# The expert gates' inverse root and exponential: from GpSimd's power to ScalarE's Sqrt and Exp

## The chip, the cores and the metric

One core of a Trainium2 chip. The program is one launch that computes two layers of a network on 8192 tokens of 256 channels. The metric is the device time of one execution in microseconds (us), smaller is better.

## The reference, cut to what matters

Each of the two layers ends with a feed-forward part in which a graph attention scores four experts for every token, and the two best experts are mixed:

```python
agg = segment_sum(msg, dst).reshape(M, HEADS * NUM_EXPERTS) + b_gat
scores = _layernorm(agg, ln_gamma, ln_beta).reshape(M, HEADS, NUM_EXPERTS).mean(1)
# _layernorm: (x - mu) * rsqrt(var + LN_EPS) * g + b      LN_EPS = 1e-5
topk_s, topk_i = jax.lax.top_k(scores, TOP_K)             # TOP_K = 2 of 4
w = jax.nn.softmax(topk_s, axis=-1)
for ei in range(NUM_EXPERTS):
    g = jnp.where(topk_i == ei, w, 0.0).sum(-1)
    hh = jax.nn.gelu(x @ W1[ei] + b1[ei], approximate=False)
    out = out + g[..., None] * (hh @ W2[ei] + b2[ei])
x = x + out
```

The change touches two values of this: 1 / sqrt(var + 1e-5), one number per token, and the exponential in the softmax over two scores, exp(second - best), one number per token. With 8192 tokens on 128 partitions each is a tile of 128 x 64.

## The kernel before

The program runs an attention layer (names at_), a feed-forward part (l0_ in the code, l_ in the profile), a convolution (cv_) and a second feed-forward part (l1_, again l_ in the profile). Each engine has its own instruction stream, written out by hand; semaphores order them, and an engine that waits holds back everything behind the wait in its stream.

A feed-forward part (ffn_layer) treats 16 blocks of 512 tokens and 4 experts, so 64 pairs of block and expert. A pair is four quarters of work. On TensorE a quarter is `up(k, q, m)` (one fourth of the hidden units of pair k, into the two PSUM banks l_pu) and, one pair behind, `down(k - 1, q, m)` (128 tokens of the pair before, into the two banks l_pd; two quarters fill one bank). ScalarE does `gelu` for each quarter of up, `fill` (writes the bias b2 into a free bank l_pd, once for each two quarters) and, for most pairs, `evict` and a store to the DRAM buffer ys. These pairs are spread over the stages in which VectorE sorts edges and merges messages, and over the loop over windows of messages (Fori on n_win).

The tail of each layer comes after that loop. VectorE divides the sums, forms mean and variance of 16 values per token (acc, var), multiplies with the inverse root (rstd2), ranks the four experts (beats, best, second, v1 = second - best), turns the exponential v2 into two weights and writes gates. With gates it combines:

- the 14 stored blocks (L1881): expert outputs l_yb, read back from ys, times gates, added to l_xo, the block's x. The SP queue loads l_xo and l_yb into a ring of three buffers, GpSimd's queue stores each block (L1061), and a buffer is loaded again once its store has landed;
- the 8 direct pairs (L1890): they are the last two blocks' pairs, whose down products stay in PSUM and are multiplied with gates and added to l_xd straight from the bank. VectorE frees a bank by s_ev, on which `fill` waits.

TAIL_ORDER alternates direct pairs and stored blocks: direct 0, stored 0, direct 1, stored 1 and 2, and so on. In the tail TensorE and ScalarE run `experts(36, ...)`, quarters z = 0 to 35 of the direct pairs, where z = 4k + q. At z, TensorE issues up of pair k and down of pair k - 1, and ScalarE the gelu of pair k, and at odd z a fill. up at z waits for the gelu of z - 2; down at the first quarter of a pair waits for all four gelus of its pair. The fill of z = 5 waits until VectorE has emptied the first bank of direct pair 0, so before the gates exist ScalarE can get as far as the gelu of z = 5 and TensorE as far as z = 7.

The two values of the change are computed by GpSimd, with var raised to -0.5 and the constant e raised to v1:

```python
pool.wait_ge(s_var, 1)
pool.tensor_tensor(rstd2, var, nhalf, ALU.pow).then_inc(s_rstd, 1)
pool.wait_ge(s_dif, 1)
pool.tensor_tensor(v2, euler, v1, ALU.pow).then_inc(s_ex, 1)
```

VectorE signals s_var (L1841) and waits for s_rstd in front of L1843; it signals s_dif (L1865) and waits for s_ex in front of L1867. All these small tiles are views of l_pay. nhalf and euler are filled by two memsets (L1826, L1827) at the start of VectorE's tail.

Of the kernel before, what the change touches and what calls it, by code (L numbers as in the profile page):

```python
# [704 lines left out]
def ffn_layer(nc, tag, x_in, x_out, w, consts, tT, ys, hs_rows, found, more):  # L705

    with ExitStack() as ctx:
# [101 lines left out]
        with ExitStack() as em:  # L809
# [40 lines left out]
        t4, s4, beats, is1, is2 = (spare[:, NT * GE * k:NT * GE * k + NT * GE].rearrange("p (t f) -> p t f", f=GE) for k in range(5))  # L850
        mean, var, rstd2, nhalf, c1, c2, best, second, v1, v2, euler = (
            spare[:, NT * GE * 5 + NT * k:NT * GE * 5 + NT * k + NT] for k in range(11))

# [159 lines left out]
        def _(pool):  # L1013
# [18 lines left out]
            with pool.Fori(0, n) as m:  # L1032
# [20 lines left out]
                pool.sem_inc(s_pgo, 1)  # L1053
            pool.wait_ge(s_var, 1)
            pool.tensor_tensor(rstd2, var, nhalf, ALU.pow).then_inc(s_rstd, 1)
            pool.wait_ge(s_dif, 1)
            pool.tensor_tensor(v2, euler, v1, ALU.pow).then_inc(s_ex, 1)
            for i, (kind, t) in enumerate(TAIL_ORDER):
# [206 lines left out]
        def _(act):  # L1265
# [47 lines left out]
            def experts(n, begin, end, m=None):  # L1313
                for z in range(at[0], at[0] + n):
                    k, q = begin + z // 4, z % 4
                    if k < end:
                        gelu(k, q, m)
                    if begin < k <= end and q % 2 and m is not LAST:
                        evict(k - 1, q // 2, m)
                    if k < end and q % 2:  # L1320
                        fill(k, q // 2, m)
                at[0] += n
# [57 lines left out]
            at[0] = 0  # L1380
            experts(4 * (PAIRS - PRE_PAIRS - LOOPED) + 4, PRE_PAIRS + LOOPED, PAIRS, LAST)
            act.wait_ge(s_comb, len(TAIL_ORDER))

        @block.vector
        def _(dve):
            steps = [0]

            def then(ins):
                steps[0] += 1
                ins.then_inc(s_vec, 1)  # L1390
                dve.wait_ge(s_vec, steps[0])
# [433 lines left out]
            steps[0] = 0  # L1825
            then(dve.memset(nhalf, -0.5))  # L1826
            then(dve.memset(euler, float(np.e)))  # L1827
            then(dve.tensor_scalar(t4, den, 1e-16, None, ALU.add))
# [12 lines left out]
            dve.nop().then_inc(s_var, 1)  # L1841
            dve.wait_ge(s_rstd, 1)
            then(dve.tensor_tensor(acc, acc, over(rstd2, GF), ALU.mult))  # L1843
            then(dve.tensor_tensor(acc, acc, vec[:, 1:2, :].to_broadcast([P, NT, GF]), ALU.mult))
# [357 lines left out]
```

## Time and profile before

| | us |
|---|---|
| median of three runs | 4274.07 |
| the three runs | 4278.59, 4269.31, 4274.07 |
| the profiled execution, its time | 4267.88 |
| its span in the profile | 4266.1 |
| busy, PE (TensorE) | 3538.0 |
| busy, DVE (VectorE) | 3012.3 |
| busy, ACT (ScalarE) | 1493.1 |
| busy, POOL (GpSimd) | 1365.0 |

The profile is of one execution. An instruction has a start and a duration, a gap in front of it is put down to what released it. Busy time is summed over the whole program, so the shares say little of a stretch of 200 us; the tails of the two layers lie at about 2440 to 2635 and 4068 to 4266 us of the span, and what sets the time there is read from the timeline of these stretches. PE rows of the experts come in groups: four records make one up, eight make one down.

### The profile page before, as it was taken

The numbers are of one execution on the slowest core, as the hardware profiler recorded it, in microseconds if no ns is written. First come the engines' busy times: TensorE is split into PE (matmuls) and PEld (weight loads), VectorE is DVE, ScalarE is ACT, GpSimd is POOL, SyncE is SP. The second block draws the span as 40 slices with busy tenths as digits, with TensorE's granted clock in tenths as the row PEclk, the third lists the DMA queues.
The fourth block names the chain that finished last, engine by engine and source line by source line (L and its number), as shares of the span: only waits on it lengthen the run. The fifth ranks groups of instructions, "written<-read, shape, count | busy, mean of one in ns | idle before, by whom it ended". The sixth has DMA issues, their size and how long they took to land. (4 is left out here: it accounts for less than half of the span.)

```text
span 4266.1 us, 51323 instructions
## 1 busy us (share of the span) xinstructions
PE 3538.0 (83%) x17914; PEld 2017.7 (47%) x17914; DVE 3012.3 (71%) x6268; ACT 1493.1 (35%) x2075; POOL 1365.0 (32%) x1016
## 2 busy tenths in 40 slices
PE   5999999999958977888798963786987888799866
PEld 2333333333316643556565642565653555565544
DVE  2676677667748887869993267858887778993357
ACT  2565556556534420222333310313520122233321
POOL 2776676667740000000274521000000000076520
PEclk9999999999978999888899987786999888899988
DMA  3000000000025200000124356126300000024247
GB/s 139 11 30 19 12 30 21 11 31 30 21 83 195 87 27 15 30 30 26 43 58 51 109 203 255 60 67 212 127 37 15 25 25 31 31 58 52 62 173 286
DMA packets 144854, 301.56 MB, mean 71 GB/s; under 512 B 20580, under 2 KB 103140, under 8 KB 139492
## 3 DMA queue, kind: packets, MB, share of 16 engines
q1 hardware_dynamic: 98212, 180.78, 11.8%
q10 hardware_dynamic: 25920, 94.38, 5.8%
q0 software_dynamic: 20480, 23.14, 4.0%
q8 instruction: 157, 2.57, 0.3%
q14 instruction: 85, 0.70, 0.1%
HBM read 183.42 MB, written 114.81 MB: 70 GB/s over the span
## 5 line engine op out<-in xcount | busy, mean ns | idle before, releaser
L1095 PE MATMUL l_pu<-l_tt,l_w 128*128 128x512 f32 x2048 | 1008.3, 617 | 116.4 <-ACT l_hid L1285 103.4
L1106 PE MATMUL l_pd<-l_w,l_hid 128*128 128x256 f32 x4096 | 971.7, 381 | 9.6 <-ACT l_hid L1285 9.6
L1106 PEld LDWEIGHTS l_pd<-l_w,l_hid 128*128 128x128 f32 x4096 | 784.6, 192 | 330.6 <-issue 247.5
L1285 ACT ACTIVATE l_hid<-l_pu,l_b 128x512 f32<-128x512 f32 x512 | 350.1, 687 | 1237.9 <-PE l_pu L1095 1227.8
L1040 POOL DMA_INDIRECT l_g<-hs_rows,l_i_src x336 | 321.6, 957 | 1304.8 <-DVE l_i_src L1655 1203.0
L389 DVE TENSOR_TENSOR at_pr<-at_ps,at_decay 128x1024 f32<-128x1024 f32 x512 | 601.0, 1216 | 177.8 <-PE at_ps L503 176.7
L307 ACT ACTIVATE at_ab<-at_pr 128x1024 f32<-128x1024 f32 x512 | 537.1, 1055 | 436.0 <-DVE at_pr L389 384.7
L258 POOL TENSOR_TENSOR at_ab<-at_ab 128x1024 f32<-128x1024 f32 x256 | 600.8, 2371 | 175.3 <-ACT at_ab L307 175.3
L1095 PEld LDWEIGHTS l_pu<-l_tt,l_w 128*128 128x128 f32 x2048 | 400.3, 200 | 418.3 <-issue 396.6
L503 PE MATMUL at_ps<-at_qr,at_kr 32*128 32x512 f32 x2048 | 348.1, 642 | 13.9 <-issue 9.0
L522 PE MATMUL at_ps_av<-at_pr,at_v 128*32 128x512 f32 x2048 | 272.9, 604 | 6.9 <-ACT at_o L315 5.1
L542 PE MATMUL at_ps<-at_xnT,at_wt 128*128 128x512 f32 x512 | 239.7, 611 | 6.8 <-DVE at_t L410 4.1
L1310 ACT ACTIVATE l_pd<-l_b 128x512 f32<-128x512 f32 x256 | 153.9, 601 | 216.2 <-DVEq L1894 165.5
L1159 PE MATMUL l_ph<-l_one_hi,l_one_lo 128*128 128x64 bf16 x2208 | 111.0, 225 | 132.1 <-DVE l_one_hi L1477 132.1
L1592 DVE SCALAR_TENSOR_TENSOR l_sent<-l_pr,l_one 128x128 f32<-128x128 f32 x360 | 84.8, 285 | 191.7 <-PE l_pr L1179 191.7
L503 PEld LDWEIGHTS at_ps<-at_qr,at_kr 32*128 32x128 f32 x2048 | 106.2, 183 | 230.1 <-issue 164.2
L1299 ACT ACTIVATE l_yst<-l_pd 128x512 f32<-128x512 f32 x224 | 133.7, 597 | 216.2 <-PE l_pd L1106 216.2
L1477 DVE TENSOR_TENSOR l_one_lo<-l_iota,l_lo 128x4096 bf16<-128x4096 bf16 (+1 forms) x72 | 158.3, 2198 | 67.9 <-PE l_ph L1159 67.0
L1881 DVE SCALAR_TENSOR_TENSOR l_xo<-l_yb,l_gates,l_xo 128x256 f32<-128x256 f32 x448 | 187.3, 481 | 19.3 <-DMA l_yb<-ys 11.5
L1159 PEld LDWEIGHTS l_ph<-l_one_hi,l_one_lo 128*128 128x128 bf16 x2208 | 102.7, 120 | 141.1 <-DVE l_one_hi L1477 139.7
L542 PEld LDWEIGHTS at_ps<-at_xnT,at_wt 128*128 128x128 f32 x512 | 93.1, 192 | 155.9 <-issue 127.6
L534 PE MATMUL at_ps_dn<-at_ab,at_roots 128*32 128x512 f32 x1024 | 141.4, 625 | 28.4 <-POOL at_ab L258 28.3
(341 smaller groups left out, 4216.7 us busy)
## 6 DMA issues: line engine op xcount, KB each, us to landing
ys<-l_yst ACTq DMA_DIRECT2D x112, 512.0 KB, 2.6
l_yb<-ys SPq DMA_DIRECT2D x28, 2048.0 KB, 10.1
l_tt<-tT ACTq DMA_DIRECT2D x36, 512.0 KB, 3.4
at_xt<-in_x SPq DMA_DIRECT2D x16, 1024.0 KB, 5.1
l_xt<-x SPq DMA_DIRECT2D x32, 512.0 KB, 4.1
tT<-l_xnT ACTq DMA_DIRECT2D x32, 512.0 KB, 4.5
l_xo<-x SPq DMA_DIRECT2D x28, 512.0 KB, 4.5
x<-at_xt SPq DMA_DIRECT2D x8, 1024.0 KB, 4.3
```

The lines of the kernel that those rows point to most:

```text
L258: pool.tensor_tensor(size(2 * k, p), size(2 * k, p), size(2 * k + 1, p), ALU.add).then_inc(s_sum, 1)
L307: act.activation(size(n // 2, n % 2), pr[:, n % 4, :, :], ACT.Abs).then_inc(s_a, 1)
L389: dve.tensor_tensor(pr[:, n % 4, :, :], ps[slot("s", n)][:, :, :], decay[:, h:h + 2, first:first + HALF], ALU.mult).then_inc(s_ring[slot(" ...
L503: ins = pe.matmul(ps[slot("s", n)][:, jj, :], kr[rows, hq, P * kb:P * kb + P], qr[rows, hq, HALF * qn:HALF * qn + HALF], start=True, stop= ...
L522: ins = pe.matmul(ps_av[KD * j:KD * j + KD, :], v[:, kb, KD * h:KD * h + KD], pr[:, (2 * u + j // 2) % 4, j % 2, :], start=(kb == 0), stop ...
L542: ins = pe.matmul(ps[slot(what, i)][:, s, :], wt[:, 2 * (i // 2) + s, k, P * hq:P * hq + P], xnT[:, k, HALF * (i % 2):HALF * (i % 2) + HAL ...
L1040: pool.indirect_dma_start(g[:, j, :], None, hs_rows[:, :], bass.IndirectOffsetOnAxis(ap=i_src[:, j:j + 1].bitcast(U32), axis=0)).then_inc( ...
L1095: ins = pe.matmul(ps_u[q % 2][:, :], w1[:, e, c, P * q:P * q + P], tt[:, s, c, :], start=(c == 0), stop=(c == KK - 1))
L1106: ins = pe.matmul(out, hid[:, k % 2, c, P * r:P * r + P], w2[:, k % GE, c, :], start=False, stop=(c == MB - 1), skip_group_check=True)
L1159: ins = pe.matmul(hist, one_lo[:, q % 2, j, :], one_hi[:, q % 2, j, :], start=False, stop=False, skip_group_check=True)
L1285: act.activation(hid[:, k % 2, q, :], ps_u[q % 2][:, :], ACT.Gelu, bias=b1[:, k % GE, q:q + 1]).then_inc(s_act, 1)
L1881: ins = dve.scalar_tensor_tensor(xo[:, b, r, :], yb[:, b, MTT * q + r, :], gates[:, MTT * t + r, q:q + 1], xo[:, b, r, :], ALU.mult, ALU.add)
```

## The change

GpSimd's two powers go. ScalarE takes the square root of var (a new tile deviation, where nhalf was) and the exponential of v1, at two places inside its stream of the direct pairs: the root behind the quarters z = 0 and 1, the exponential behind z = 2, 3 and 4. VectorE takes the reciprocal of the root (L1843 of the changed kernel) and no longer fills the two constants. The semaphores are the same four, now waited on and signalled by ScalarE.

```diff
-        mean, var, rstd2, nhalf, c1, c2, best, second, v1, v2, euler = (
-            spare[:, NT * GE * 5 + NT * k:NT * GE * 5 + NT * k + NT] for k in range(11))
+        mean, var, rstd2, deviation, c1, c2, best, second, v1, v2 = (
+            spare[:, NT * GE * 5 + NT * k:NT * GE * 5 + NT * k + NT] for k in range(10))
...
-            pool.wait_ge(s_var, 1)
-            pool.tensor_tensor(rstd2, var, nhalf, ALU.pow).then_inc(s_rstd, 1)
-            pool.wait_ge(s_dif, 1)
-            pool.tensor_tensor(v2, euler, v1, ALU.pow).then_inc(s_ex, 1)
...
-            experts(4 * (PAIRS - PRE_PAIRS - LOOPED) + 4, PRE_PAIRS + LOOPED, PAIRS, LAST)
+            experts(2, PRE_PAIRS + LOOPED, PAIRS, LAST)
+            act.wait_ge(s_var, 1)
+            act.activation(deviation, var, ACT.Sqrt).then_inc(s_rstd, 1)
+            experts(3, PRE_PAIRS + LOOPED, PAIRS, LAST)
+            act.wait_ge(s_dif, 1)
+            act.activation(v2, v1, ACT.Exp).then_inc(s_ex, 1)
+            experts(4 * (PAIRS - PRE_PAIRS - LOOPED) - 1, PRE_PAIRS + LOOPED, PAIRS, LAST)
             act.wait_ge(s_comb, len(TAIL_ORDER))
...
-            then(dve.memset(nhalf, -0.5))
-            then(dve.memset(euler, float(np.e)))
...
             dve.wait_ge(s_rstd, 1)
+            then(dve.reciprocal(rstd2, deviation))
             then(dve.tensor_tensor(acc, acc, over(rstd2, GF), ALU.mult))
```

ScalarE's stream at the start of the direct pairs, before. l0_hid is a gelu (its input l0_pu0 or l0_pu1 tells even and odd quarters), l0_pd0 and l0_pd1 are fills; these rows are z = 2 to z = 5, and at_op is the reused semaphore that counts ups.

```order
L1285 ACTIVATE l0_hid<-l0_pu0,l0_b1 128x512 [waits at_op]
L1273 REGISTER_ALU
L1285 ACTIVATE l0_hid<-l0_pu1,l0_b1 128x512 [waits at_op]
L1273 REGISTER_ALU
L1310 ACTIVATE l0_pd1<-l0_b2 128x512 [waits l0_s_ev]
L1273 REGISTER_ALU
L1285 ACTIVATE l0_hid<-l0_pu0,l0_b1 128x512 [waits at_op]
L1273 REGISTER_ALU
L1285 ACTIVATE l0_hid<-l0_pu1,l0_b1 128x512 [waits at_op]
L1273 REGISTER_ALU
L1310 ACTIVATE l0_pd0<-l0_b2 128x512 [waits l0_s_ev]
```

The same engine with the change, from the gelu of z = 1 to that of z = 2 (l0_pay is the tile of the root):

```order
L1281 ACTIVATE l0_hid<-l0_pu1,l0_b1 128x512 [waits at_op]
L1269 REGISTER_ALU
L1306 ACTIVATE l0_pd0<-l0_b2 128x512 [waits l0_s_ev]
L1379 ACT_TABLE_LOAD
L1379 ACTIVATE l0_pay<-l0_pay 128x64 [waits l0_s_var]
L1269 REGISTER_ALU
L1281 ACT_TABLE_LOAD [waits at_op]
L1281 ACTIVATE l0_hid<-l0_pu0,l0_b1 128x512
```

And further on in the same stream with the change, from the fill of z = 3 over the gelu of z = 4 to that of z = 5:

```order
L1306 ACTIVATE l0_pd1<-l0_b2 128x512 [waits l0_s_ev]
L1269 REGISTER_ALU
L1281 ACTIVATE l0_hid<-l0_pu0,l0_b1 128x512 [waits at_op]
L1382 ACT_TABLE_LOAD
L1382 ACTIVATE l0_pay<-l0_pay 128x64 [waits l0_s_dif]
L1269 REGISTER_ALU
L1281 ACT_TABLE_LOAD [waits at_op]
L1281 ACTIVATE l0_hid<-l0_pu1,l0_b1 128x512
L1269 REGISTER_ALU
L1306 ACTIVATE l0_pd0<-l0_b2 128x512 [waits l0_s_ev]
```

Two activations and four table loads have come in between gelus that stood next to each other. The loads for the root and the exponential stand ahead of their waits, the loads for the gelu behind them. TensorE's and SP's streams are unchanged, and GpSimd's loses the two powers and an instruction that belongs to them.

## Rows read from the trace of the kernel before

**Rows 1.** The page's first row: the span of the profiled execution.

```profile
span 4266.1 us, 51323 instructions
```

**Rows 2.** The chain that ended last, 4060:4266.1 (layer 1's tail), shares by line.

```profile
by line: DVE l_xo L1881 29.4%; issue 9.0%; PE l_pu L1095 8.6%; PE l_pd L1106 7.4%; POOL l_pay L1055 5.2%; POOL l_pay L1057 5.1%; DMA l_yb<-ys 5.1%; DVE l_xd L1890 4.3%; DMA out<-l_xo 4.1%; DVE l_pay L1857 1.1%; DVE l_pay L1856 1.1%; DVE l_p
```

**Rows 3.** Lines 1055 and 1057: who waited for each (us in total, times).

```profile
  DVE l_rows L1843: 21.6, 2
...
  DVE l_pay L1867: 21.4, 2
```

**Rows 4.** Timeline, layer 0's gates: start, duration, instruction, idle before and releaser.

```profile
2440.61 0.11 DVE L1826 MEMSET l_pay<- 128x64 f32 x1 [1.17 <-DVE l_state L1816]
...
2440.95 0.29 DVE L1828 TENSOR_SCALAR l_pay<-l_state 128x256 f32<-128x256 f32 x1
...
2451.05 0.20 DVE L1840 TENSOR_SCALAR l_pay<-l_pay 128x64 f32<-128x64 f32 x1
...
2451.39 10.61 POOL L1055 TENSOR_TENSOR l_pay<-l_pay 128x64 f32<-128x64 f32 x1 [22.93 <-DVEq L1841]
...
2462.03 1.23 DVE L1843 TENSOR_TENSOR l_rows<-l_rows,l_pay 128x1024 f32<-128x1024 f32 x1 [10.79 <-POOL l_pay L1055]
...
2476.73 0.22 DVE L1864 TENSOR_TENSOR l_pay<-l_pay 128x64 f32<-128x64 f32 x1
...
2487.68 0.20 DVE L1867 TENSOR_SCALAR l_pay<-l_pay 128x64 f32<-128x64 f32 x1 [10.72 <-POOL l_pay L1057]
...
2490.47 0.88 DVE L1890 SCALAR_TENSOR_TENSOR l_xd<-l_pd,l_gates,l_xd 128x256 f32<-128x256 f32 x2 [0.37 <-DVE l_gates L1872]
...
2491.67 0.88 DVE L1890 SCALAR_TENSOR_TENSOR l_xd<-l_pd,l_gates,l_xd 128x256 f32<-128x256 f32 x2 [0.33 <-DVE l_xd L1890]
...
2492.79 6.80 DVE L1881 SCALAR_TENSOR_TENSOR l_xo<-l_yb,l_gates,l_xo 128x256 f32<-128x256 f32 x16 [0.24 <-DVE l_xd L1890]
```

**Rows 5.** The same timeline: ScalarE and TensorE around the gates.

```profile
2446.82 1.31 ACT L1285 ACTIVATE l_hid<-l_pu,l_b 128x512 f32<-128x512 f32 x2
...
2463.21 1.89 PE L1106 MATMUL l_pd<-l_w,l_hid 128*128 128x256 f32 x8
...
2492.87 3.75 PE L1095 MATMUL l_pu<-l_tt,l_w 128*128 128x512 f32 x4 [27.77 <-ACT l_hid L1285]
```

**Rows 6.** ScalarE's timeline at an earlier exponential; one Sqrt, one RECIPROCAL (ns).

```profile
2099.20 1.28 ACT L1355 ACT_TABLE_LOAD   x1
2103.47 0.63 ACT L1355 ACTIVATE l_ye<-l_ym 128x512 f32<-128x512 f32 x1 [2.99 <-DVE l_ym L1715]
2104.11 1.28 ACT L1285 ACT_TABLE_LOAD   x1
2105.41 0.69 ACT L1285 ACTIVATE l_hid<-l_pu,l_b 128x512 f32<-128x512 f32 x1
...
L1332 ACT ACTIVATE l_sd<-l_ve x32: 205/205/206, 1270.8 to 3043.9; 128x4 f32<-128x4 f32 x32
...
L1868 DVE RECIPROCAL l_pay<-l_pay x2: 553/553/553, 2487.9 to 4115.9; 128x64 f32<-128x64 f32 x2
```

**Rows 7.** TensorE's timeline after pauses: next quarter at 2498.37, and a shorter pause.

```profile
2498.37 1.88 PE L1095 MATMUL l_pu<-l_tt,l_w 128*128 128x512 f32 x4
...
2562.31 3.35 PE L1095 MATMUL l_pu<-l_tt,l_w 128*128 128x512 f32 x4 [5.29 <-ACT l_hid L1285]
...
2565.50 1.89 PE L1106 MATMUL l_pd<-l_w,l_hid 128*128 128x256 f32 x8
```

**Rows 8.** VectorE's timeline: the two banks of direct pair 1.

```profile
2502.13 0.88 DVE L1890 SCALAR_TENSOR_TENSOR l_xd<-l_pd,l_gates,l_xd 128x256 f32<-128x256 f32 x2 [2.54 <-PE l_pd L1106]
...
2509.01 0.88 DVE L1890 SCALAR_TENSOR_TENSOR l_xd<-l_pd,l_gates,l_xd 128x256 f32<-128x256 f32 x2 [6.01 <-PE l_pd L1106]
```

**Rows 9.** Two stretches of 10 us: busy time of each engine, PEclk, DMA share, GB/s.

```profile
2455.00:2465.00 10.00, 10.00 (x36) 6.46 (x34) 2.90 (x3) 0.69 (x1) 7.00 (x1) 1.00 0.97 392
2465.00:2475.00 10.00, 0.10 (x1) 0.00 (x0) 9.14 (x26) 0.00 (x0) 0.00 (x0) 0.73 0.02 8
```

## The prediction, on record before the changed kernel ran

> **What bounds the kernel now.** I read the chain that ended last first, in the tail of layer 1: VectorE's combining of stored blocks leads with 29.4%, and GpSimd's two powers hold 5.2% and 5.1% of a window of 206 us [rows 2], so they are on the path that sets the end. The lines' own views show why: VectorE waits for them 21.6 us over the two layers for the root and 21.4 for the exponential [rows 3]. Then the timeline of layer 0's gates. VectorE ends L1840 at 2451.25 and goes on at 2462.03; it ends L1864 at 2476.95 and goes on at 2487.68; the root alone takes GpSimd 10.61 [rows 4]. The first direct combine, which needs gates, starts at 2490.47. Last I looked at what else could be late: TensorE ends its last quarter before the gates at 2465.10, and stands 27.77 us until VectorE frees the first bank [rows 5]; the DMA queues moved 8 GB/s between 2465 and 2475 [rows 9], after 392 in the ten before, so the loads that were out, the first three stored blocks, had landed by then. Nothing but VectorE's gate arithmetic holds this stretch, and a microsecond less there should be a microsecond less at the end of the layer.
>
> **The change part by part.** All for one layer; layer 1 repeats it, since the two waits differ by nothing there [rows 3].
>
> *Memsets.* L1826 starts at 2440.61 and L1828 at 2440.95 [rows 4]: -0.34. s_var comes at 2451.25 - 0.34 = 2450.91.
>
> *The root.* Before: 2462.03 - 2451.25 = 10.78 from the end of L1840 to L1843. With the change: signal to the other engine 0.14 (2451.25 to 2451.39, rows 4), the Sqrt, the signal back, and a reciprocal. No row has a Sqrt of 64 columns: 4 columns take 0.205 us, and the exponential of 512 takes 0.63 [rows 6]; the line between the two gives 0.26 at 64. For the signal back I take 0.10, between 0.03 (GpSimd's end at 2462.00 to VectorE at 2462.03) and 0.14. The reciprocal of 128 x 64 is 0.55 [rows 6], and the step to the next instruction 0.03. Sum 1.08, so -9.70.
>
> *The exponential.* Before 2487.68 - 2476.95 = 10.73; after 0.14 + 0.26 + 0.10 = 0.50; -10.23.
>
> *Table loads.* Four more per layer, 1.28 each. Those of the root and the exponential stand ahead of their waits in the stream, and in such a place the load ran while the engine would have waited: at 2099.20, with its exponential at 2103.47 [rows 6]. Here ScalarE's second gelu ends at 2448.13 [rows 5]; a fill, shorter than a gelu (0.69), and the load bring it to 2450.1, before s_var at 2450.91. The load for the exponential falls into about 11 us of waiting. If one were not covered it would cost 1.28. The two gelu loads are paid by ScalarE, and then perhaps by TensorE.
>
> *What queues behind the waits.* This is the part that could eat the gain. Behind the root's wait stand the gelus of z = 2 and 3, which needed nothing from VectorE before. The root ends at 2451.31, the load at 2452.60, the gelu of z = 2 at 2453.3; TensorE's z = 4 waits for it and can't start before. Its quarters take 3.44 at full clock (the two banks of pair 1 are filled 2509.01 - 2502.13 = 6.88 apart, two quarters, rows 8), so z = 4, 5 and 6 end at 2463.6. Still harmless.
>
> Behind the exponential's wait stands the gelu of z = 5, for which z = 7 waits: up of pair 1, and behind it the down that fills the second bank of direct pair 0. v1 is ready at 2476.95 - 0.34 - 9.70 = 2466.91; exponential to 2467.31, load to 2468.60, gelu to 2469.29, TensorE at 2469.4. After 27.77 us of pause four records of up took 3.75, where 1.88 is full speed, and the next quarter started 5.50 after the first [rows 5, 7]; after a pause of 5.29 it was 3.35, and the down ended 5.1 after the start [rows 7]. TensorE's pause here is 5.8 us, so I take 5.1 to 5.5: second bank ready at 2474.5 to 2474.9.
>
> VectorE's first combine starts at 2490.47 - 20.27 = 2470.20 and the second would at 2471.40. **So a new wait of about 3 us appears in front of the second combine of direct pair 0.** I expect it to cost nothing in the end. Before, z = 8 started cold at 2492.87 and z = 9 at 2498.37 [rows 5, 7]; moved by 20.27 these are 2472.60 and 2478.10. With the change z = 8 follows z = 7 at once, on a warmed clock: 2474.5 to 2474.9 plus 3.44 is 2477.9 to 2478.3. The slow quarter is paid once in either kernel, only earlier. VectorE has room as well: it would reach the first bank of pair 1 some 8.25 us after starting that second combine (2491.67 before; stored block 0 ends at 2499.59, and a step of 0.33 follows, rows 4), at 2483.1, where TensorE has it at 2502.13 - 20.27 = 2481.86. That is 1.3 late, and the next wait, 6.01 at 2509.01 [rows 8], takes it in. From there the two kernels run alike.
>
> A rule that speaks against this change: the Trainium skill, ScalarE: Activation LUTs, section What ACT_TABLE_LOAD costs, has each change of table set at 1283 ns of load plus about 1380 ns of drain, 2.66 us in all. This trace agrees on the load and shows no drain: it begins 0.01 after the exponential's end at 2104.10 and the gelu follows 0.02 behind it [rows 6]. By the page the quarter z = 5 would come 1.4 us later than worked out above, and the sum would lose up to that much per layer.
>
> *Sum.* -0.34 - 9.70 - 10.23 = -20.27 per layer, -40.5 in all. From the bounds: a function between 0.21 and 0.63, a signal back between 0.03 and 0.14, four of each, give -41.0 to -38.9. The profiled execution took 4267.88, with 1.8 outside its span [rows 1]: 4227.3. It is the fastest of four executions; the median of the runs is 4274.07, and the mean of all four 4272.5. From that mean: **4232 us**.
>
> **The rivals.**
>
> *A, the forecast:* 4232. Chance 0.77.
>
> *B, the new wait isn't absorbed.* TensorE comes to z = 7 cold and z = 8 is slow again, or the wait passes on to the store and load of the buffer ring. If z = 8 too takes 5.50 in place of 3.44, z = 9 starts at 2474.9 + 5.5 = 2480.4, 2.3 behind; a wait paid in full is 3.1 to 3.5 (2474.5 to 2474.9 less 2471.40). So +5 to +7 in both layers, 4237 to 4239. For it: both pauses in the rows, 27.77 and 5.29, end in a slow start. Against: after each the down of the same quarter, or at the latest the next quarter, runs at full speed. 0.08.
>
> *C, a table change costs more than its load* (a drain that the rows at 2104 don't show because a gelu of 512 columns hides it): 1.4 us more at z = 5, partly absorbed, 0 to +3: 4232 to 4235. The page named above is this rule. 0.04.
>
> *D, the loads run behind the waits.* Where a register instruction stands between wait and function, they do; here the stream has none. Then +1.28 at four waits, +5.1: 4237. 0.05.
>
> *E, transfers set the tail.* Its start moves, but blocks come from the ring as late as before. Against: the queues are empty from 2465, and a stored block (2 MB of l_yb, 0.5 of l_xo, 0.5 stored) needs 8.0 us at 392 GB/s [rows 9], less than the 8.25 that VectorE takes for one and a direct bank. That is close, which is why it stands here. Time as before, 4272. 0.03.
>
> *F, the other side: slower.* ScalarE's stall of 11 us ahead of the exponential is paid in full, if TensorE's direct pairs, not the gates, set the tail. z = 7 ended at 2465.10 before and ends at about 2474.7 with the change, 9.6 later per layer: +19, 4292. It decides once TensorE has no pause at the gates; before, it has one of 27.77, so this wants 20 us that aren't there. 0.02. The rest, 0.01, is for a root or an exponential that costs many microseconds.
>
> **How the numbers follow.** A difference under about 0.2% can't be told from none here: the three runs before lie 0.22% apart. A, B, C and D are faster by 0.8 to 1.0%: 0.95 with a little of the rest. E is the same: 0.03. F is slower: 0.02. The range takes A to D, from 4239 in B up to 4242 with part of the runs' spread (about 5 either way), and down to 4225, a little under the profiled execution's own 4227.3.
>
> **What the changed profile would show.** GpSimd with nothing between its last gather and its first store. VectorE's waits before L1843 and L1868 of the changed kernel at about 0.5 us each, released by ScalarE. Sqrt and Exp of 128 x 64 at 0.26; the table loads ahead of them with no idle time behind the wait. The first direct combine 29.6 us after the start of VectorE's tail (2490.47 - 2440.61 = 49.86 before, less 20.27), the second waiting about 3 us for TensorE; TensorE's pause at the gates split, one of about 6 us before z = 7, and none worth naming before z = 8. From the first bank of pair 1 on, all distances as before.
>
> The prediction is wrong if the waits for ScalarE are over 2 us, if TensorE is slow beyond one quarter, or if the tail behind the gates grows by what the gates lost.

## The result, and the profile of the changed kernel

| kernel | median, us | all runs, us | profiled span, us |
|---|---|---|---|
| before | 4271.69 (4 runs) | 4267.49 to 4278.59 | 4266.1 |
| changed | 4240.78 (4 runs) | 4238.91 to 4243.07 | 4237.0 |

The ratio is 0.9926, with a 95% interval of 0.9909 to 0.9944: 30.9 us faster by the medians, 29.1 by the profiled spans. The forecast was 4232 with a range of 4225 to 4242, so the range holds the result, but 40.5 us were promised and some 9 of them are missing. That the range holds it is luck: its upper part was there for rival B, which did not come, and what did happen had no term in the sum. The next rows show that the missing time is not where the change was made.

The changed kernel's timeline on VectorE at layer 0's gates (start, duration, instruction, idle before it and releaser), which answers to [rows 4, 8]:

```profile
2446.06 0.29 DVE L1828 TENSOR_SCALAR l_pay<-l_state 128x256 f32<-128x256 f32 x1 [1.12 <-DVE l_state L1818]
...
2456.16 0.20 DVE L1840 TENSOR_SCALAR l_pay<-l_pay 128x64 f32<-128x64 f32 x1
2456.73 0.55 DVE L1843 RECIPROCAL l_pay<-l_pay 128x64 f32<-128x64 f32 x1 [0.38 <-ACT l_pay L1379]
...
2472.70 0.20 DVE L1868 TENSOR_SCALAR l_pay<-l_pay 128x64 f32<-128x64 f32 x1 [0.38 <-ACT l_pay L1382]
2475.49 0.88 DVE L1891 SCALAR_TENSOR_TENSOR l_xd<-l_pd,l_gates,l_xd 128x256 f32<-128x256 f32 x2 [0.37 <-DVE l_gates L1873]
2480.79 0.88 DVE L1891 SCALAR_TENSOR_TENSOR l_xd<-l_pd,l_gates,l_xd 128x256 f32<-128x256 f32 x2 [4.43 <-PE l_pd L1102]
2481.91 6.80 DVE L1882 SCALAR_TENSOR_TENSOR l_xo<-l_yb,l_gates,l_xo 128x256 f32<-128x256 f32 x16 [0.24 <-DVE l_xd L1891]
2489.04 0.88 DVE L1891 SCALAR_TENSOR_TENSOR l_xd<-l_pd,l_gates,l_xd 128x256 f32<-128x256 f32 x2 [0.33 <-DVE l_xo L1882]
2494.57 0.88 DVE L1891 SCALAR_TENSOR_TENSOR l_xd<-l_pd,l_gates,l_xd 128x256 f32<-128x256 f32 x2 [4.65 <-PE l_pd L1102]
```

The two waits of 10.8 and 10.7 us are 0.38 each. The first direct combine comes 29.43 us behind L1828 (49.52 before; 49.52 less 20.27 and with the memsets' 0.34 back gives the forecast's 29.59). A new wait of 4.43 stands ahead of the second one. At the second bank of pair 1 the changed kernel is 19.08 us behind its first combine, and the kernel before 18.54 [rows 4, 8]: of the new wait 0.54 is left. In layer 1 these distances are 19.38 and 18.63, so 0.75 is left, and the wait is:

```profile
4094.98 0.88 DVE L1891 SCALAR_TENSOR_TENSOR l_xd<-l_pd,l_gates,l_xd 128x256 f32<-128x256 f32 x2 [4.73 <-PE l_pd L1102]
```

ScalarE and TensorE in the same stretch, which answers to [rows 5, 6]:

```profile
2454.66 1.28 ACT L1379 ACT_TABLE_LOAD   x1
2456.44 0.26 ACT L1379 ACTIVATE l_pay<-l_pay 128x64 f32<-128x64 f32 x1 [0.50 <-DVEq L1841]
2456.72 1.28 ACT L1281 ACT_TABLE_LOAD   x1
2458.01 1.26 ACT L1281 ACTIVATE l_hid<-l_pu,l_b 128x512 f32<-128x512 f32 x2
...
2461.63 1.28 ACT L1382 ACT_TABLE_LOAD   x1
2472.41 0.26 ACT L1382 ACTIVATE l_pay<-l_pay 128x64 f32<-128x64 f32 x1 [9.50 <-DVEq L1866]
2472.68 1.28 ACT L1281 ACT_TABLE_LOAD   x1
2473.98 0.69 ACT L1281 ACTIVATE l_hid<-l_pu,l_b 128x512 f32<-128x512 f32 x1
...
2467.52 1.89 PE L1102 MATMUL l_pd<-l_w,l_hid 128*128 128x256 f32 x8
2474.81 3.75 PE L1091 MATMUL l_pu<-l_tt,l_w 128*128 128x512 f32 x4 [5.40 <-ACT l_hid L1281]
2478.35 2.29 PE L1102 MATMUL l_pd<-l_w,l_hid 128*128 128x256 f32 x8
2480.48 1.88 PE L1091 MATMUL l_pu<-l_tt,l_w 128*128 128x512 f32 x4
```

Both loads that stand ahead of a wait had ended before the wait did, the root's by only 0.50 us (0.30 in layer 1), and the gelu's load begins 0.01 us after the function's end with its gelu 0.02 behind it: 1.28 us and nothing more. TensorE stands 5.40 us, runs one quarter slowly (its four up records take 3.75), and the next up is at 1.88 again.

The missing time turns up in the convolution, so its names are needed. It treats eight quarter images one behind the other. For each, VectorE takes mean and variance (cv_stats, cv_ve), GpSimd raises cv_ve to -0.5 (cv_rstd), VectorE normalises (cv_xn) and takes the largest absolute value (cv_amax), GpSimd spreads the maximum over the partitions (an all-reduce, cv_aall), and VectorE makes the scale cv_s_lhs of it and the rounded cv_q, with which TensorE goes on. So one cv_s_lhs marks one quarter image.

To find the missing 9 us I cut both profiled executions at the same instructions of VectorE and compared the pieces (us; each is the difference of two starts read from the timelines):

| piece | before | changed | |
|---|---|---|---|
| all up to layer 0's tail | 2440.95 | 2446.06 | +5.11 |
| tail of layer 0 (L1828 to the first cv_stats) | 201.64 | 182.26 | -19.38 |
| convolution: first cv_stats to the first cv_s_lhs | 18.38 | 21.88 | +3.50 |
| first to last cv_s_lhs | 169.82 | 173.06 | +3.24 |
| last cv_s_lhs to the start of layer 1 | 58.58 | 58.73 | +0.15 |
| layer 1 up to its tail | 1179.56 | 1177.88 | -1.68 |
| tail of layer 1 (to the end) | 197.17 | 177.13 | -20.04 |

The tails gained 39.4 us, as forecast. The piece up to layer 0's tail differs from one execution of the same kernel to the next (2682.1 and 2691.9 us in late_root's two profiles, below), so its +5.1 proves nothing. The convolution is steadier, and it gave back 6.9. The changed kernel's timeline at its first quarter image, GpSimd and VectorE:

```profile
2622.54 0.10 POOL L1978 MEMSET cv_nhalf<- 128x8 f32 x1 [6.86 <-POOLq L41]
...
2635.56 1.68 POOL L1969 TENSOR_TENSOR cv_rstd<-cv_ve,cv_nhalf 128x8 f32<-128x8 f32 x1 [11.06 <-issue]
...
2631.74 0.17 DVE L2033 TENSOR_SCALAR cv_ve<-cv_mv 128x8 f32<-128x8 f32 x1
2637.28 2.67 DVE L2038 TENSOR_SCALAR cv_xn<-cv_xt,cv_mv,cv_rstd 128x256 f32<-128x256 f32 x8 [5.36 <-POOL cv_rstd L1969]
```

cv_ve is ready at 2631.91, and GpSimd begins the power at 2635.56: 3.65 us in which it isn't waiting for VectorE ("issue"). The lines' own views say what it does. The changed kernel, L1969:

```profile
L1969 POOLq MODIFY_POOL_CONFIG  x16: 38/83/98, 2624.2 to 2798.2; - x16
L1969 POOL TENSOR_TENSOR cv_rstd<-cv_ve,cv_nhalf x8: 1682/1692/1693, 2635.6 to 2809.0; 128x8 f32<-128x8 f32 x8
```

The kernel before, the same line (there L1968), and L1055, the gates' root:

```profile
L1968 POOLq MODIFY_POOL_CONFIG  x14: 83/83/98, 2661.9 to 2805.8; - x14
...
L1055 POOLq MODIFY_POOL_CONFIG  x4: 11/12/12, 2440.7 to 4068.3; - x4
L1055 POOL TENSOR_TENSOR l_pay<-l_pay x2: 10607/10608/10608, 2451.4 to 4079.4; 128x64 f32<-128x64 f32 x2
```

GpSimd changes its configuration (two records a time) when a power follows instructions of another sort. Before, that stood ahead of the gates' root, issued at 2440.7, where GpSimd would have waited for s_var until 2451.39; the convolution's first power found it done and its line had 14 records. With the gates' powers gone the line has 16. The change of configuration, called the switch from here on, moved into the convolution, is issued at 2624.2, right behind the memsets, and the power starts 11.4 us later. GpSimd's stream shows the same. Before, from the last gather's branch to the convolution's first power (the ISA row is the switch):

```order
218 L1055 ISA
219 L1055 TENSOR_TENSOR l_pay<-l_pay 128x64
...
233 L1983 MEMSET cv_pad 128x4x32
234 L1968 TENSOR_TENSOR cv_rstd<-cv_ve,cv_nhalf 128x8
```

With the change, the same place:

```order
230 L1984 MEMSET cv_pad 128x4x32
231 L1969 ISA
232 L1969 TENSOR_TENSOR cv_rstd<-cv_ve,cv_nhalf 128x8
```

The row that stood ahead of the gates' root stands ahead of the convolution's now.

### The profile page after: what moved, and what is told of

It reads as the page before. It is cut to its first block and busy times, and to the rows that moved or that the text cites. A ratio compares the mean times of both kernels' runs of the same rounds, so it can differ in the third digit from the quotient of the medians.

```text
span 4237.0 us, 51327 instructions
## 1 busy us (share of the span) xinstructions
PE 3556.5 (84%) x17914; PEld 2024.1 (48%) x17914; DVE 3012.9 (71%) x6266; ACT 1504.8 (36%) x2087; POOL 1323.1 (31%) x1012
## 5 line engine op out<-in xcount | busy, mean ns | idle before, releaser
L307 ACT ACTIVATE at_ab<-at_pr 128x1024 f32<-128x1024 f32 x512 | 537.0, 1055 | 437.4 <-DVE at_pr L389 400.9
L534 PE MATMUL at_ps_dn<-at_ab,at_roots 128*32 128x512 f32 x1024 | 139.7, 618 | 23.3 <-POOL at_ab L258 23.2
```

The lines of the kernel that those rows point to most:

```text
L307: act.activation(size(n // 2, n % 2), pr[:, n % 4, :, :], ACT.Abs).then_inc(s_a, 1)
```

## The experiments

Theory S, as first put: the switch costs the 3.5 us of the wait ahead of the first cv_xn, and the rest of the missing time is scatter. Rival N, as put for again: all 9 us are systematic; as put for dummy_power: the wait is scatter. All ratios are against the kernel before on the same chip. The first four ran on one chip, where the kernel before took 4274.07 us; the other eight on a chip where it took 4761.72 and 4763.05. There the looped pairs are longer (from layer 0's last node block to its tail 1264 to 1270 us in place of 1020 to 1024) and the convolution and the tails are within 2.5 us of those on the first chip, so tails and convolutions are compared across both, within that, and times only within one. The kernel before has no profile on the second chip.

**again**: the changed kernel unchanged.

> The changed kernel once more, as the bar for the others. In its profile the two tails are 19.7 and 20.4 us shorter than before (40.1, against 40.5 forecast), but the whole span is only 29.1 shorter. Theory S (switch): 3.5 us of the difference are real and sit at the first root of the convolution (VectorE waits 5.36 there instead of 1.85), because GpSimd's ISA instruction that goes ahead of a power had been carried out in the tail, under a wait, and is now carried out in the convolution; the other 7 or so are scatter of stages with TensorE's clock (attention +2.6, exchange +2.5, convolution's later blocks +3.2, edge lists -1.2). Then this run lies 37 us (33 to 40) under the kernel before in other executions. Rival N: all 9 us are systematic, and it lies 31 under (30 to 32) again.

Measured: 4240.97 (4240.77 to 4245.04), ratio 0.9927 [0.9913, 0.9941]. The gain is 33.1, the wait ahead of the first cv_xn 6.33, the tails 182.6 and 177.8. That is at the edge of what theory S expected and beyond rival N's 30 to 32, so it decides for neither. But 7.4 of the 40.5 us are missing again, and the convolution takes 253.8 again (253.7 in the first profile): most of the shortfall repeats.

**dummy_power**: a power of one column that nobody needs, at the place of the two removed.

```diff
+            pool.wait_ge(s_primed, 1)
+            pool.tensor_tensor(primed[:, :], primed[:, :], primed[:, :], ALU.pow).then_inc(s_primed, 1)
             for i, (kind, t) in enumerate(TAIL_ORDER):
```

> The changed kernel, and GpSimd raises a 128 x 1 tile of ones to itself behind its last gather, for which nobody waits. Theory S: the first power of the convolution has no ISA instruction of its own in front any more, VectorE's wait there is 1.85 again, and the time is 3.5 us under that of the changed kernel. Rival N (the wait of 5.36 is scatter of the barrier or of the loads ahead of it): wait and time as in the changed kernel, 0.

Measured: 4232.63 (4229.21 to 4236.66), ratio 0.9905 [0.989, 0.9921]. Its timeline in the tail and at the convolution's start:

```profile
2449.73 0.76 POOL L1057 TENSOR_TENSOR l_primed<-l_primed 128x1 f32<-128x1 f32 x1 [20.87 <-issue]
...
2626.92 1.68 POOL L1973 TENSOR_TENSOR cv_rstd<-cv_ve,cv_nhalf 128x8 f32<-128x8 f32 x1 [7.51 <-DVE cv_ve L2037]
...
2628.64 2.67 DVE L2042 TENSOR_SCALAR cv_xn<-cv_xt,cv_mv,cv_rstd 128x256 f32<-128x256 f32 x8 [1.88 <-POOL cv_rstd L1973]
```

A useless instruction makes the kernel 8.3 us faster by the medians. GpSimd's power starts as soon as cv_ve is there, its line is back at 14 configuration records, VectorE's wait is 1.88 again, and the convolution takes 247.1 in place of 253.7. So the wait isn't scatter. But 8.3 is more than the 3.5 to 4.5 of the wait, so S as put was too small: the later quarter images belong to it too (170.3 from the first to the last cv_s_lhs, against 172.4 and 173.1).

**root_only** and **exp_only**: one of the two functions on ScalarE, the other still a power of GpSimd.

```diff
# root_only
+            pool.wait_ge(s_dif, 1)
+            pool.tensor_tensor(v2, euler, v1, ALU.pow).then_inc(s_ex, 1)
# exp_only
+            pool.wait_ge(s_var, 1)
+            pool.tensor_tensor(rstd2, var, nhalf, ALU.pow).then_inc(s_rstd, 1)
```

> Only the root goes to ScalarE, the exponential stays GpSimd's power. By the terms of the prediction: -0.17 (one memset) and -9.70 per layer, 19.7 us in all under the kernel before, and since a power is left in the tail no 3.5 us in the convolution (theory S). Without that theory this run and exp_only share what the whole change brings, 31: about 15 each.

> Only the exponential goes to ScalarE, the root stays GpSimd's power. By the terms: -0.17 and -10.23 per layer, 20.8 us in all under the kernel before, with the power's ISA instruction in the tail, so nothing lost in the convolution. Theory S wants root_only and exp_only together at -40.5; the rival (not additive for another reason) at -31.

Measured: root_only 4249.5 (4247.77 to 4258.44), 0.9952 [0.9938, 0.9966]; exp_only 4252.67 (4244.28 to 4255.71), 0.9947 [0.9933, 0.996]. Each still has a power in the tail, and each has a wait of 1.86, with a convolution of 247.4 and 248.0. Layer 0's tail is 9.9 and 10.3 shorter, 20.2 together, against 19.4 for both at once. In layer 1 it is 10.8 and 9.8, 20.5 together, against 20.0. So the halves add up in the tails to within 0.8 us and not in the time, 24.6 + 21.4 by the medians (20.5 + 22.7 by the ratios, each within about 6) against 33. The medians' 46.0 are more than the 40.5 that theory S wanted, within that scatter; the rival's 31 is out. What is lost comes only when the last power has gone.

**exp_behind_gelu5**: the exponential one gelu later, so that TensorE has its input.

```diff
+            gelu(PRE_PAIRS + LOOPED + 1, 1, LAST)
             act.wait_ge(s_dif, 1)
             act.activation(v2, v1, ACT.Exp).then_inc(s_ex, 1)
-            experts(4 * (PAIRS - PRE_PAIRS - LOOPED) - 1, PRE_PAIRS + LOOPED, PAIRS, LAST)
+            fill(PRE_PAIRS + LOOPED + 1, 0, LAST)
+            at[0] += 1
+            experts(4 * (PAIRS - PRE_PAIRS - LOOPED) - 2, PRE_PAIRS + LOOPED, PAIRS, LAST)
```

> The exponential of the gates stands on ScalarE behind the gelu that followed it, the second of pair 1, so TensorE has its input before ScalarE begins to wait for the denominators; the table load of the next gelu stands one gelu later. The wait of 4.4 to 4.7 us ahead of the second combine should go. Theory A (that wait is taken up behind the second and third combine, where VectorE waited for TensorE anyway): the tails grow no shorter; the load of 1.3 us now stands on ScalarE ahead of a later gelu, so 0 to 1.3 us per layer worse, 0 to +2.6 us in all against the changed kernel. Theory B (that wait is paid for): 3 to 4.4 us per layer better, 6 to 9 in all, and the tails 177 to 179 and 173 to 174 us in place of 182.3 and 177.1.

Measured: 4733.7 (4729.72 to 4734.38), 0.9938 [0.9925, 0.9952], 28.0 under before; the changed kernel on this chip (again_b, below) 28.1. VectorE's direct combines in layer 0:

```profile
2720.92 0.88 DVE L1894 SCALAR_TENSOR_TENSOR l_xd<-l_pd,l_gates,l_xd 128x256 f32<-128x256 f32 x2 [0.37 <-DVE l_gates L1876]
2722.13 0.87 DVE L1894 SCALAR_TENSOR_TENSOR l_xd<-l_pd,l_gates,l_xd 128x256 f32<-128x256 f32 x2 [0.33 <-DVE l_xd L1894]
...
2734.22 0.88 DVE L1894 SCALAR_TENSOR_TENSOR l_xd<-l_pd,l_gates,l_xd 128x256 f32<-128x256 f32 x2 [4.18 <-PE l_pd L1102]
2741.10 0.87 DVE L1894 SCALAR_TENSOR_TENSOR l_xd<-l_pd,l_gates,l_xd 128x256 f32<-128x256 f32 x2 [6.01 <-PE l_pd L1102]
```

The new wait is gone, and it is paid for: the wait of 0.33 at pair 1's first bank is 4.18, that of 4.65 at the second 6.01. Its second bank comes 20.18 us behind the first combine, against 19.32 to 19.73 in the seven other profiles on this chip, and the tails take 185.3 and 180.7, against 182.9 to 184.7 and 177.2 to 178.9. Theory B, by which the tails grow shorter, falls. The tails are 1.4 and 2.6 us over the mean of the seven, in one profile, a little more than theory A's 0 to 1.3 per layer; the time shows no difference. The wait of 4.4 us cost almost nothing where it stood, and to take it away in this way gains nothing.

**late_root**: dummy_power with a delay of two powers, and no switch, in the convolution.

```diff
+            pool.wait_ge(s_ve, 1)
+            pool.tensor_tensor(idle[:, :], ve[:, :], nhalf[:, :], ALU.pow).then_inc(s_idle, 1)
+            pool.wait_ge(s_idle, 1)
+            pool.tensor_tensor(idle[:, :], ve[:, :], nhalf[:, :], ALU.pow).then_inc(s_idle, 1)
             root(0)
```

> This kernel is dummy_power with two more powers of 128x8 by GpSimd into a tile that nobody reads, behind the convolution's first cv_ve and ahead of its first cv_rstd. So the first quarter image is held up by 2 x 1.7 = 3.4 us, about what the changed kernel's switch of GpSimd holds it up, and there is no switch. Every theory expects VectorE's wait ahead of the first cv_xn at 1.9 + 3.4 = 5.3 us. Theory S (the switch costs its own wait, and the delay that it makes moves the later quarter images to a worse place in TensorE's clock, which costs 2 to 3 us more): from the first to the last cv_s_lhs 172 to 173 us in place of 170.3, and the time 5 to 7 us over dummy_power, so 4238 to 4240. Theory T (the later 2 to 3 us have nothing to do with the delay; something else in the changed kernel makes them): 170 to 171 us between them, and 3.4 us over dummy_power, about 4236.

Measured: 4728.02 (4718.61 to 4730.27), 0.9926 [0.9912, 0.9939]. The wait is 5.19, the first cv_s_lhs comes 21.71 us after the start, as late as in the changed kernel (21.88), and from the first to the last it is 170.5. That speaks for theory T, but it was one profile.

**conv_root**: the convolution's eight roots on ScalarE too, so that GpSimd has no power there.

```diff
+            def root(b):
+                act.wait_ge(s_ve, b + 1)
+                act.activation(deviation[:, :], ve[:, :], ACT.Sqrt).then_inc(s_rstd, 1)
...
                 dve.wait_ge(s_rstd, b + 1)
+                then(dve.reciprocal(rstd[:, :], deviation[:, :]))
...
             for b in range(B):
                 padded(b)
+                if b + 1 < B:
+                    root(b + 1)
```

> The changed kernel, with the convolution's eight inverse roots from ScalarE's Sqrt and VectorE's reciprocal too, ScalarE's behind its copies for the quarter image before. GpSimd has no power left in the convolution. Theory S: with no power GpSimd needs no switch there, neither ahead of the first one nor between each power and each all-reduce; the wait ahead of the first cv_xn goes from 5.4 to under 1.5 us, the wait of each all-reduce behind its cv_amax grows shorter by about 1 us, and the time is 8 to 12 us under the changed kernel's, 4229 to 4233. Rival L (ScalarE comes late, since its copies for the quarter image before take 6.6 us and stand ahead of the root): 1 to 2 us more for each of 7 quarter images, which gives back 7 to 14 us, so about the changed kernel's time or up to 4 us over it.

Measured: 4720.82 (4718.63 to 4727.81), 0.9915 [0.9902, 0.9929], 40.9 under before, the changed kernel on this chip (again_b) 28.1. From the start of the convolution to the first cv_s_lhs 17.03 us, then 169.15. The all-reduces start 2.4 us behind the start of their cv_amax from the first image on; with powers that is so from the third on, so only the first two gain by it. Rival L has its mechanism right and its price wrong: from the fourth image on VectorE waits 2.5 to 2.7 us for ScalarE's root, but the distances from one cv_s_lhs to the next, 23.7 to 23.9 us there, are no longer than in the changed kernel (23.9).

**conv_root_once**: only the first of these roots on ScalarE.

> The changed kernel, with the first of the convolution's eight inverse roots alone from ScalarE's Sqrt and VectorE's reciprocal; GpSimd's first power is that of the second quarter image, for which it has some 20 us of idle time before. Theory S: the switch is still there, but hidden; the wait ahead of the first cv_xn is under 1.5 us in place of 5.4, and the time is that of dummy_power or up to 2 us better, 4230 to 4233. Rival: the switch costs as much wherever it stands, since it holds GpSimd's stream up and the first all-reduce with it: about the changed kernel's time, 4239 to 4241.

Measured: 4724.44 (4717.45 to 4729.79), 0.9923 [0.991, 0.9937], 37.3 under before. The first cv_s_lhs comes 17.03 us after the start, so the first wait is gone, the switch is hidden in GpSimd's idle time before the second power, and from the first to the last cv_s_lhs it takes 171.7. The rival, that the switch costs as much wherever it stands, falls. Yet its convolution takes 247.8, no less than dummy_power's 247.1 and 247.3, though its first image is 1.35 us sooner.

**again_b, dummy_power_b, late_root_b, conv_root_b**: the four kernels that matter most, unchanged, on one chip.

> The changed kernel, unchanged, beside the next three on one chip. In two profiled executions before, it took 173.1 and 172.4 us from the first to the last cv_s_lhs of the convolution, and five executions without the switch ahead of the convolution's first power took 169.8 to 171.2. Both theories expect 172 to 173 here, a wait of 5.4 to 6.6 us ahead of the first cv_xn, and 30 to 33 us under the kernel before.

> dummy_power, unchanged. Both theories expect a wait of 1.9 us ahead of the first cv_xn, 170 to 171 us from the first to the last cv_s_lhs, and 7 to 9 us under the changed kernel.

> late_root, unchanged: no switch, but its delay of 3.4 us. Theory T (the delay alone costs what it takes, and the 2 us more of the later quarter images go with the switch by another way): 170 to 171 us from the first to the last cv_s_lhs, as in its first profile (170.5), and 3 to 4 us over dummy_power. Theory S (the delay sets where TensorE's clock rises in the later quarter images, and the first profile was an outlier): 172 to 173 us, and 5 to 7 us over dummy_power.

> conv_root, unchanged, now on one chip with the changed kernel. By its first profile the first cv_s_lhs comes 17.0 us behind the start of the convolution in place of 21.9 (dummy_power: 18.4), and 169.2 us lie between the first and the last: 8 to 10 us under the changed kernel and 1 to 2 us under dummy_power. Rival: the later quarter images come back to 171 to 172 us, and it is level with dummy_power.

| kernel | median, us | ratio | to first cv_s_lhs | first to last |
|---|---|---|---|---|
| again_b | 4734.96 (4723.54 to 4737.46) | 0.9936 [0.9922, 0.995] | 23.54 | 172.54 |
| late_root_b | 4730.93 (4728.52 to 4733.94) | 0.9933 [0.9919, 0.9947] | 21.70 | 170.78 |
| dummy_power_b | 4728.63 (4726.68 to 4731.1) | 0.993 [0.9916, 0.9944] | 18.39 | 170.47 |
| conv_root_b | 4717.27 (4708.65 to 4722.54) | 0.9906 [0.9892, 0.992] | 17.04 | 168.62 |

The first cv_xn in again_b, late_root_b and conv_root_b, with the instruction that releases it:

```profile
2883.11 1.68 POOL L1969 TENSOR_TENSOR cv_rstd<-cv_ve,cv_nhalf 128x8 f32<-128x8 f32 x1 [12.49 <-issue]
2884.82 2.67 DVE L2038 TENSOR_SCALAR cv_xn<-cv_xt,cv_mv,cv_rstd 128x256 f32<-128x256 f32 x8 [7.02 <-POOL cv_rstd L1969]
```

```profile
2883.56 1.64 POOL L1974 TENSOR_TENSOR cv_rstd<-cv_ve,cv_nhalf 128x8 f32<-128x8 f32 x1
2885.24 2.67 DVE L2047 TENSOR_SCALAR cv_xn<-cv_xt,cv_mv,cv_rstd 128x256 f32<-128x256 f32 x8 [5.19 <-POOL cv_rstd L1974]
```

```profile
2862.32 1.28 ACT L1990 ACT_TABLE_LOAD   x1 [40.01 <-PEq L41]
2871.48 0.21 ACT L1990 ACTIVATE cv_deviation<-cv_ve 128x8 f32<-128x8 f32 x1 [7.87 <-DVE cv_ve L2032]
2871.72 0.20 DVE L2036 RECIPROCAL cv_rstd<-cv_deviation 128x8 f32<-128x8 f32 x1 [0.27 <-ACT cv_deviation L1990]
```

A delay of 3.3 us without a switch costs 3.6 us in the convolution (250.98 against 247.34; 2.3 by the medians) and leaves the later images at 170.5 and 170.8, as theory T has it. But late_root's delay is the smallest of the delays in question: its first cv_s_lhs is 3.33 us later than in the kernel before, those of the four profiles with the switch exposed are 3.50, 4.47, 4.73 and 5.16 later. Theory T stands for 3.33 us; for the longer ones theory S is not tested. The changed kernel is 6.3 us over dummy_power_b by the medians, a little under the 7 to 9 expected, and 7.2 over it in the convolution alone (254.55 against 247.34). The changed kernel's wait is itself not constant: 5.36, 6.33, 6.59 and 7.02 in four executions of kernels with the switch there. conv_root_b is 17.7 us under again_b by the medians, more than the 8 to 10 expected; the convolution has 10.5 of them (244.01), and most of the rest lies ahead of layer 0's tail, where executions of one kernel differ as much. It is the version that beats both kernels here: 45.8 us under the kernel before, and 40.9 in its first run, where the changed kernel (again_b) has 28.1, a little under the 30 to 33 expected.

**The root's table load on the second chip.** Part of that smaller gain is in the tails. again_b at layer 0's root, ScalarE and VectorE:

```profile
2701.70 1.28 ACT L1379 ACT_TABLE_LOAD   x1
2702.99 0.26 ACT L1379 ACTIVATE l_pay<-l_pay 128x64 f32<-128x64 f32 x1
...
2701.37 0.20 DVE L1840 TENSOR_SCALAR l_pay<-l_pay 128x64 f32<-128x64 f32 x1
2703.28 0.55 DVE L1843 RECIPROCAL l_pay<-l_pay 128x64 f32<-128x64 f32 x1 [1.72 <-ACT l_pay L1379]
```

The load starts after VectorE has finished the variance (2701.57), so here nothing hides it, and VectorE stands 1.72 us in place of 0.38. In all eight profiles on this chip it stands 1.2 to 2.4 us there, in both layers. ScalarE comes late because the gelus of z = 0 and 1 stand ahead of the load and wait for TensorE: the gelu's own table load comes 5.3 us behind L1828 in the changed kernel's profile and 7.2 behind it in again_b. On the first chip the load had ended only 0.06 to 0.54 us before the root began (the changed kernel, again and dummy_power, both layers).

**The later quarter images.** What differs between the changed kernel and dummy_power is when TensorE's clock rises. Here is the stretch from 40 to 45 us behind the first cv_q in the changed kernel and in dummy_power (busy time of each engine, PEclk, DMA share, GB/s):

```profile
2694.00:2699.00 5.00, 5.00 (x32) 3.79 (x31) 2.99 (x10) 0.00 (x0) 0.00 (x0) 0.64 0.00 0
```

```profile
2685.00:2690.00 5.00, 5.00 (x42) 4.28 (x41) 4.38 (x13) 0.00 (x0) 0.00 (x0) 0.88 0.00 0
```

TensorE is busy throughout in both and gets 32 matmuls done at a mean granted clock of 0.64, 42 at 0.88: a mix of its two levels, 1.2 and 2.4 GHz. Cut to the hundredth from the first cv_q (the rows are cut to whole microseconds), this stretch, picked after the fact, puts all fourteen profiles in the order of their later images: 1.00 and 0.99 (conv_root_b, conv_root) go with 168.6 and 169.2 us, 0.93 (before) with 169.8, 0.79 to 0.88 (the two profiles each of dummy_power and late_root, root_only and exp_only) with 170.3 to 171.2, 0.74 (conv_root_once) with 171.7, 0.71 (exp_behind_gelu5) with 172.0, 0.66, 0.65 and 0.60 (again, again_b, changed) with 172.4, 172.5 and 173.1.

Part of this order is a coincidence. conv_root's two profiles gain their time from the first cv_s_lhs to the second (29.5 us, against 31.5 to 31.8 in all others), ahead of this stretch; from the second to the last they take 139.6 and 139.1, more than the kernel before (138.3). In the other twelve the order holds from the second to the last too, from 138.3 us at 0.93 to 141.4 at 0.60, but for 0.04 us. Most of the difference is in two images: from the second cv_s_lhs to the third the four profiles with the switch exposed take 21.2 to 21.7 us, the seven others with a power ahead of the first image 20.2 to 20.8, and from the third to the fourth it is 23.7 to 24.0 against 23.2 to 23.5. From the fourth on all lie within 0.5 us for each image.

The trace also gives the rise itself: the second time that the granted clock rises to its upper level behind the first cv_stats. It is at 62.5 to 63.9 us in before, dummy_power's two, root_only and exp_only, at 66.5 and 66.8 in late_root's two, and at 69.3 to 70.4 in the four with the switch exposed. So late_root's delay of 3.33 us moved it by 3.5 and 3.6 us against dummy_power's two, and the changed kernel's delay of 3.50 by 6.3. Either the rise jumps somewhere between these two delays, or the switch acts by another way; a kernel without the switch and with a delay of 4 to 5 us would tell, and was not run.

## Why the prediction was right, and where it was 9 us off

*The root and the exponential*: right. From the end of L1840 (2456.36) to the start of the instruction behind the reciprocal (2457.32) it is 0.96, forecast at 1.08. Ahead of L1868 VectorE stands 0.38, forecast 0.50. Before, it stood 10.8 and 10.7 us.

*Table loads*: right here, with less room than was worked out. The loads of both functions ran before their waits ended (D falls), but the root's had 0.50 and 0.30 us to spare where the forecast had 0.8 (2450.1 against 2450.91). The forecast took the time of ScalarE's second gelu from the kernel before as fixed to VectorE's tail; it is set by TensorE's first quarters and moves against it. On the second chip the load is exposed, wholly or in part, and VectorE's wait there passed the forecast's own limit of 2 us in four of eight profiles, all of kernels with the same root (2.24 to 2.41 in layer 0). The gelu's load starts 0.01 us after the function's end, where there was no gelu of 512 columns to hide a drain (C falls). By the rule of the Trainium skill, ScalarE: Activation LUTs, section What ACT_TABLE_LOAD costs, with its drain of about 1380 ns, that gelu would have started at about 2475.4; it started at 2473.98, so the measurement decides against the drain here.

*What queues behind the waits*: right in its mechanism, off in a size. The wait ahead of the second combine was put at 3.1 to 3.5 and measured 4.43 and, in layer 1, 4.73. TensorE took z = 7 up at 2474.81, where the forecast's 2469.4 and the later start of the tail (2446.06 - 2440.61 = 5.45) give 2474.9; what was too small is the quarter behind it. It was taken at 5.1 to 5.5 and took from 2474.81 to about 2480.7, 5.9; its down took 2.29 in place of 1.89. That most of it is absorbed was argued before, and is shown by the distances (0.54 and 0.75 us left of it) and by exp_behind_gelu5. From the first bank of pair 1 on the distances were to be as before; that bank is 1.9 us later (13.55 against 11.66), and the second 0.54. B falls.

*E and F*: the tails are 19.4 and 20.0 us shorter, so neither the transfers nor TensorE set their end.

*The sum*: -40.5 for the tails was -39.4. The step that failed has no term in it: the section on the change has GpSimd's stream lose "the two powers and an instruction that belongs to them", and the prediction gives that loss no cost anywhere else. The instruction, GpSimd's switch, was not theirs alone; the convolution's first power used it. Taking its user away moved it from a place where GpSimd waits for VectorE anyway to a place in the convolution where VectorE waits for GpSimd. It measures +3.5 us (5.2 in again_b) to the first cv_s_lhs, and the later images are 2.1 to 3.2 longer than in dummy_power or the kernel before. dummy_power, which takes the switch back out of the convolution, lies at 4232.63, the forecast's 4232; so close a match is luck, since its tails gained 38.6 and not 40.5. By the profiles -39.4 + 6.9 = -32.5, against -30.9 and -33.1 by the medians. The shift could be read beforehand in GpSimd's order of instructions, at a place outside the lines of the diff. The Trainium skill, GPSIMD Engine Reference, section Instruction dispatch, says that the first call to a freshly loaded GpSimd kernel pays about 6 us (5.95 measured there, from the MODIFY_POOL_CONFIG to the call) with no instruction visible in the profile. This trace agrees on the kind and not on the size: issued at 2624.2, the switch would, as an estimate by the page's figure, be done at 2630.2, ahead of cv_ve at 2631.91, and cost nothing; the power started at 2635.56, 11.4 us behind it.

*What stays open.* That the exposed switch goes with some 2 us more in the later images is shown by four profiles with it (172.0 to 173.1) against nine without (168.6 to 171.2). By which way isn't shown: late_root's two rule out a delay of 3.33 us and no longer one, and conv_root_once, whose first image is sooner and whose switch is hidden, still takes 171.7, in one profile, which speaks for the place at which the clock rises and not for the switch as such. The link from the granted clock to the time of these images is an order of profiles, not an experiment in which the clock alone was changed.

## What to carry to other kernels

An instruction that is removed takes with it what the compiler put ahead of it, and a later instruction may live on that: compare the order of instructions of the whole program on that engine, not only at the edit, and price each generated instruction at its new place by what waits there. If the last GpSimd power of a stage goes, let the next stage's go too, or keep a cheap one where GpSimd idles. A table load ahead of a wait is free only as long as the engine gets there early enough; what stands ahead of it in the stream, and what that waits for, sets the room. And a new wait is worth its own time only if nothing behind it on that engine waits for the same producer: compare distances from a fixed instruction further down, not the wait.

## What the runs showed of the hardware

- GpSimd's change of configuration costs far more than its records show (0.01 to 0.1 us each): behind the convolution's memsets the first power started after 11.1 to 12.5 us of "issue" in four executions of kernels that have it there, and the one-column power in the tail 8.4 us after its records (2441.3 to 2449.73).
- It goes both ways: with powers ahead of all images of the convolution the first all-reduce starts 3.6 to 6.4 us after the start of its cv_amax, the second 3.0 to 3.4, the later ones 2.4; without them (conv_root) all start after 2.4.
- A Sqrt of 128x64 takes 0.26 us and VectorE's reciprocal 0.55, where GpSimd's power took 10.61; at 128x8 it is 0.21 and 0.20 against 1.69.
